# Six instead of three projection matmuls between a step's scores and its weighing

## The reference

```python
x = x + attn(layernorm(x), wq, wk, wv, wo)     # 32 heads of 64, 8 key/value heads, rotary, causal
x = x + xattn(layernorm(x), ctx_2048)          # both sides rounded to fp8 by blocks, then x @ ctx^T
x = x + moe(layernorm(x), Wg, W1, W3, W2, sw1, sw3, sw2)   # 8 experts, top 1, capacity 256, one shared
```

```python
xq, xk, xv = x @ wq, x @ wk, x @ wv            # then rotary on xq and xk
scores = einsum('bqhd,bkhd->bhqk', xq, xk) / 8, with a causal mask
out = einsum('bhqk,bkhd->bqhd', softmax(scores), xv) @ wo
```

## Time and profile before

| | |
|---|---|
| median of three runs | 1614.04 us (1612.98 to 1614.66) |
| the profiled execution | 1614.8 us, of which span 1613.0 us |
| mean granted TensorE clock | 0.956 of full speed (2.4 GHz) |
| TensorE matmul busy | 1467.1 us, 91% |
| VectorE / ScalarE / GpSimd busy | 1237.6 (77%) / 917.9 (57%) / 1058.6 us (66%) |
| attention, step 0 | from 51.73 us |
| steps 52 to 59 | 422.33 to 495.87 us |
| step 117 | from 912.21 us |

### The profile page before, as it was taken

One profiled execution on the slowest core, in us unless ns is written; L12 is line 12 of the kernel. 1 busy time (PEld: TensorE's weight loads), 2 busy tenths in 40 slices (PEclk: granted clock), 3 DMA queues, 4 the chain that ended last, 5 costly groups with the idle time before them and its releaser, 6 DMA issues.

```text
span 1613.0 us, 26858 instructions
## 1 busy us (share of the span) xinstructions
PE 1467.1 (91%) x8616; PEld 1290.2 (80%) x8616; DVE 1237.6 (77%) x2986; ACT 917.9 (57%) x2277; POOL 1058.6 (66%) x1040
## 2 busy tenths in 40 slices
PE   5899999999989999999999967728889898899997
PEld 4688888888878888888888856627778787899996
DVE  6787787788887787788787879858797964677785
ACT  2587777777667777777777655422121213566562
POOL 1798888888776888888888767626252522444545
PEclk9899999999999999999999988969989899899998
DMA  5322232222312222232322333031101003577767
GB/s 189 87 73 66 81 76 71 77 81 55 81 50 63 75 74 66 81 89 55 82 76 59 112 119 92 8 125 41 52 27 53 7 27 113 160 234 221 226 209 239
DMA packets 78796, 152.13 MB, mean 94 GB/s; under 512 B 15366, under 2 KB 15622, under 8 KB 78656
## 3 DMA queue, kind: packets, MB, share of 16 engines
q1 hardware_dynamic: 76096, 142.16, 30.3%
q0 software_dynamic: 2560, 8.25, 1.5%
HBM read 87.58 MB, written 16.78 MB: 65 GB/s over the span
## 4 chain that ended last, share of the span: by engine, by line
PE 74%; DVE 12%; issue 6%; POOL 4%; ACT 2%; DMA 1%; SPq 1%; DVEq 0%; POOLq 0%; ACTq 0%
PE bank L400 15%; PE bank L401 15%; PE bank L402 15%; PE bank L442 7%; PE bank L418 5%; PE bank L457 5%; PE bank L458 5%; PE bank L419 4%; PE bank L392 2%; DVE work L943 1%; POOL P L1390 1%; DVE work L1056 1%; DVE aam L1095 1%; PE bank L429 1%; DVE st L938 1%
## 5 line engine op out<-in xcount | busy, mean ns | idle before, releaser
L742 ACT ACTIVATE P<-P,mn 128x512 f32<-128x512 f32 (+3 forms) x512 | 284.5, 556 | 221.6 <-DVE mn L994 220.9
L1390 POOL TENSOR_TENSOR P<-P,ri 128x128 f32<-128x128 f32 (+3 forms) x512 | 353.9, 724 | 10.4 <-DVE ri L983 10.4
L994 DVE CUSTOM_DVE_ANT_0 P<-bank,mask 128x512 f32<-128x512 f32 (+3 forms) x512 | 235.6, 479 | 118.3 <-PE bank L419 117.9
L1035 DVE TENSOR_TENSOR PTl<-bank,PTh 128x512 fp32r<-128x512 f32 (+1 forms) x384 | 229.2, 598 | 37.0 <-ACT PTh L754 33.9
L442 PE MATMUL bank<-ident,P 128*128 128x128 f32 x1280 | 203.4, 274 | 7.2 <-POOL P L1390 7.2
L754 ACT ACTIVATE PTh<-bank 128x512 fp32r<-128x512 f32 (+1 forms) x384 | 197.6, 516 | 6.0 <-PE bank L442 2.9
L418 PE MATMUL bank<-KT,QT 128*128 128x256 f32 (+2 forms) x512 | 191.2, 373 | 7.4 <-DVE mn L994 7.3
L457 PE MATMUL bank<-PTh,VS 128*128 128x256 f32 (+2 forms) x512 | 164.5, 332 | 11.5 <-DVE PTl L1035 8.8
L400 PE MATMUL bank<-XT,Wh 128*128 128x512 f32 x384 | 165.4, 431 | 9.6 <-DVE qcs L1007 4.7
L419 PE MATMUL bank<-KT,QT 128*128 128x256 f32 (+2 forms) x512 | 167.3, 327 | 0.0
L1428 POOL TENSOR_TENSOR OTl<-Opair,OTh 128x512 fp32r<-128x512 f32 x64 | 83.5, 1305 | 120.8 <-ACT OTh L764 120.5
(11 more groups left out here) (190 smaller groups left out, 4214.5 us busy)
## 6 DMA issues: line engine op xcount, KB each, us to landing
RW<-in_wf SPq DMA_DIRECT2D x170, 256.0 KB, 3.2
QT<-qh SPq DMA_DIRECT2D x256, 64.0 KB, 2.0
QT<-ql SPq DMA_DIRECT2D x256, 64.0 KB, 2.0
Wraw<-in_wqkv SPq DMA_DIRECT2D x16, 768.0 KB, 4.8
Oraw<-in_wo SPq DMA_DIRECT2D x16, 512.0 KB, 3.4
KT<-KT SPq DMA_DIRECT2D x32, 256.0 KB, 2.9
work<-in_ctx SPq DMA_DIRECT2D x32, 256.0 KB, 2.7
krot<-kvs SPq DMA_DIRECT2D x64, 64.0 KB, 2.0
```

The lines of the kernel that those rows point to most:

```text
L742: e.activation(pq, pq, ACT.Exp, bias=mn[:, z, qb:qb + 1], scale=-1.0, accum_out=rs[:, z, qb:qb + 1]).then_inc(a_exp, 1)
L994: e.tensor_tensor_reduce(P[:, z, off[qb]:off[qb] + k], bank[n % 2][:, 0:k], mask[:, 512 - k:512], -0.125, BIG, ALU.add, ALU.min, mn[:, z, ...
L1035: e.tensor_tensor(pt_part(PTl, part), bank[2 + part][:, 0:128 * n].rearrange("p (m n) -> p m n", n=128), pt_part(PTh, part).bitcast(F32), ...
L1390: e.tensor_tensor(pq, pq, ri[:, z, qb:qb + 1].to_broadcast([128, n]), ALU.mult).then_inc(g_norm, 1)
```

## The change

Of the three projection chunks of a step, nine matmuls, the kernel before issues the first (three matmuls) between `scores(h, 2)` and `weigh(h - 3)`, and the other two (six matmuls) between `turn_p(h - 2, 2)` and `attn_out(h - 7)`. The changed kernel issues two chunks at the first place and one at the second. The order of the chunks among themselves, their waits, and the work of the other engines are as they were.

```diff
--- before.py
+++ after.py
@@ -636,7 +636,8 @@
                     scores(h, 3)
                     scores(h, 2)
                 if unit < NU:
-                    project(unit, 3 * k // 4, 3 * k % 4)
+                    for at in range(3 * k, 3 * k + 2):
+                        project(unit, at // 4, at % 4)
                 if 0 <= h - 3 < NH:
                     weigh(h - 3)
                 if h >= NH - 11:
@@ -656,8 +657,7 @@
                 if 0 <= h - 2 < NH:
                     turn_p(h - 2, 2)
                 if unit < NU:
-                    for at in range(3 * k + 1, 3 * k + 3):
-                        project(unit, at // 4, at % 4)
+                    project(unit, (3 * k + 2) // 4, (3 * k + 2) % 4)
                 if 0 <= h - 7 < NH:
                     attn_out(h - 7)
                 if h < -4:
```

## The result

| | before | changed |
|---|---|---|
| median | 1614.05 us (1612.98 to 1615.16, 6 runs) | 1621.01 us (1617.99 to 1623.38, 6 runs) |
| ratio, 95% interval | | 1.0043, 1.0031 to 1.0055 (+5.0 to +8.9 us) |
| the profiled execution | 1614.8 us, span 1613.0, clock 0.956 | 1623.38 us, span 1621.6, clock 0.951 |

The change makes the kernel 7.0 us slower.

What follows compares the result with a forecast made beforehand. TensorE, busy 91%, was taken as the bound, so a new order could only create or remove waits. The terms +0.6 - 1.2 + 2.6 + 0.1 + 0.7 = +2.8 us gave 1616.8 us; range 1611.0 to 1623.0.

Steps and rivals of the forecast that it cites:

- (a): Whole kernel: the forecast case, a small sum of terms of both signs, 1614 to 1620 us; chance 0.54.
- within 0.2%: Whole kernel: a change of at most 3.2 us, 1610.8 to 1617.3, hardly told from none; chance 0.51.
- (c): Steps with k = 1, 2, 3: `join` misses `attn_out`, 81 steps pay about 0.1 us, 1624.2 in all; chance 0.17.
- part 2: Every eighth step: `weigh` no longer waits for the X add, 12 x 0.10 = -1.2 us.
- part 1: `join` to `attn_out`: tightest margin falls from 0.94 to 0.25 us, 0.02 to 0.03 lost in 26 steps, +0.6 us.
- part 3: Steps 52 to 59: the later inner group delays VectorE's X add, for which `first_turn` waits; +2.6 us.
- rival (d): Steps 52 to 59: longer waits drop the clock to 1.2 GHz, about +5 us, 1621.8; chance 0.05.
- part 4: The start: 0.70 us won by matmuls ahead of a GpSimd wait, given back in steps 3 to 8; +0.1 us.
- part 5: The end, after step 119: the chain of waits follows the inner group, so 0.69 us is paid once; +0.7 us.
- Rival (b): Steps 52 to 59 and start: VectorE's slack swallows the lateness, the start keeps its gain; -2.6 us, 1611.4; chance 0.15.
- (e): Whole kernel: the order is hidden wherever it stands, TensorE being full; 1614.0 us; chance 0.09.

Runs made afterwards that it cites:

- experiment on both places: Against the kernel before: last three projection matmuls behind `attn_out` in steps 52-59 and every eighth quiet step, VectorE's add and normalising earlier in 52-59; 1607.47 us, ratio 0.9964.
- experiment on the waiting steps: Against the kernel before: six projection matmuls ahead only in steps whose `weigh` waits for the X add (and step 2); 1618.02 us, ratio 1.0033.

## Why the prediction was right, and where not

The sign was right, and 1621.0 lies inside the whole range (1611.0 to 1623.0). It lies 1.0 above what I gave to the forecast case (a), 1614 to 1620, and 4.2 above the 1616.8 that I named; "within 0.2%", to which I gave the best chance (0.51), did not come. That the range held owes something to luck: its upper end was drawn for (c) and for a clock at half speed, and what filled it was a spacing and a late copy that stood in no term, beside a small fall of the clock. The terms, each from the profiles:

| term | predicted | measured |
|---|---|---|
| part 2, waits of `weigh` | -1.2 | -1.2 |
| part 1, what the new order costs in quiet steps | +0.6 | +2.8 |
| part 3, steps 52 to 59 (step 56 from least to least) | +2.6 | +2.2 |
| rival (d), the clock | in no sum | 1.4 to 1.6 in two of three profiles, about +1.0 |
| part 4, step 2 and steps 3 to 8 | +0.1 | +0.16 |
| the copy of the keys | in no sum | about +1.1 at step 0 (the copy itself +1.3 to +1.8) |
| part 5, the end | +0.7 | +0.5, not told from nothing |
| sum | +2.8 | about +6.6 |

Measured as a whole: +7.0 and +6.8 us. The four experiments that change one stage each sum to 2.4 + 1.8 + 2.9 - 0.1 = +7.0, of which 0.5 is the return to the old order at step 51. Each of the four is uncertain by some 1.5 us, so that they meet the whole this closely is in part luck.

**Part 1 failed in its size and in its reason.** The margins came out as worked out (0.25 predicted, 0.24 measured for k = 2), `attn_out` lost nothing by them, and rival (c) did not occur. I charged the 26 steps with the tightest margin 0.02 to 0.03 us each and put the rest at nothing. Steps with k = 0, whose margin is 0.82, take 7.74 instead of 7.70, those with k = 1 7.17 instead of 7.11 to 7.14, and the others 7.14 and 7.12 instead of 7.11: the quiet stages take +0.76 and +0.92 us (+1.6 together on average over three profiles), and with the 1.2 that part 2 gives back that is +2.8. What pays most of it is TensorE's spacing: in three kinds of step `attn_out`'s matmuls stand 0.233 us apart and not 0.228 to 0.229, which is 0.024 us a step or 1.8 us in all. The rest is spread over the step's other matmuls, most of it over the four of `scores` 3 and 2 (0.01 to 0.015 us a step where k = 0, 1 or 2). The spacing of `attn_out` does not follow VectorE's weight splits: in the step with k = 0 VectorE splits weights in every second unit only, and the spacing is the same in both. In the kind with the tightest margin (k = 2) it is the narrow one. Six or nine matmuls between the transposes and `attn_out` go with the narrow spacing throughout. Three go with the wide one in three kinds of step, but not for k = 2, and with both in the experiment on both places. So TensorE's sequence has a part in it and can't be the whole cause; the mechanism stays open. My condition for being wrong, "if quiet steps without a wait take another time than 7.1 us", was met by a few hundredths, and a few hundredths in 98 steps came to 2.8 us where I had 0.6.

The Trainium skill, "TensorE: Matmul & The Clock Gate", section "Back-to-back issue gap", gives between matmuls of 512 columns about 216 ns for one alone and about 131 ns in a stream, and no number by place. No such pair in these rows is under 0.22 us, and the 0.005 us between one place in the order and another is what counted here.

**Part 2 was right**: 7.14 us for step 18, no late matmul in `weigh`. The experiment on the waiting steps adds what the prediction left out: the gain holds only while the next step has the new order too.

**Part 3 was right by step**, 52 to 55 and 57 to 59 within 0.07 us. Step 56 costs +0.67 for +0.69 where its split is equally long, and +0.28 from least to least, since in two of the three profiles with the new order the split no longer ran beside a GpSimd instruction. I had not looked at that. The waits of `first_turn` sum to 10.9 us in the changed kernel (11.8 predicted) and to 11.9 where the split was long. The longest was to be in step 56; in the changed kernel it is the one of step 54 (1.65), and step 56 has 1.05:

```profile
PE bank L392 <- DVE X L1044: 10.9, 8, 1.6
```

That VectorE's chain sets these steps, which the +0.45 rested on, is shown by its reversal: moving the add forward in that chain gained 6 us.

**Rival (d)**, given 0.05, occurred in small, in two of three profiles: half the speed for 3.4 us, 1.4 to 1.6 us lost and not 5.

**Part 4 was right in both halves** (-0.67 for -0.70, +0.83 for +0.8) and incomplete. I followed TensorE, GpSimd and VectorE, and no DMA. The copy of the keys is late in all three profiles with the new order up to step 8 and in none of the eleven others, with a packet of instructions among its own packets each time; in the others that packet comes from 37.8 us on, behind the copy. The rest of the attention says the same: of the 64 KB copies of keys (krot) and queries (QT from qh) before 900 us, 3148 had no packet of instructions (8 KB or more) in their time, and all but one of them took 1.89 to 2.06 us; 1018 had one, and took up to 3.97, with medians of 2.3 and 2.4. So a packet among its own is what makes such a copy late. What moves the packet is open, since the one step that I blamed did not do it.

**Rival (b)** (VectorE's slack swallows the delay) and **(e)** (hidden everywhere) are out: the waits grew.

## What to carry to other kernels

When the engine that is full has its work reordered, price each place by what the *other* engine on the loop does: moving TensorE's matmuls alone won 1.6 us at best here and cost up to 89, and moving VectorE's X add and normalising with them won 5.6 us. Where a stage repeats a hundred times, compare whole steps of the same kind across margins, not only the margins: 0.03 us a step is 3 us. A reorder in some steps only can be paid again where the old order comes back (0.47 us here behind each waiting step, nothing behind step 59), so try it as a block. An instruction that is longer in one profile than in another is not chance until one has looked at what the other engines do beside it.

## What the runs showed of the hardware

- Matmuls of the same shape on a full TensorE at clock 1.00 do not all have one spacing: in `attn_out` it is 0.225 to 0.236 us by their place, and the mean of the six mostly repeats within 0.001 us from step to step (0.228 to 0.229 in the order before, 0.233 in three of four kinds of step in the changed one). What sets it is open.
- Instructions are fetched by the same DMA engines as data, 0.02 MB a packet; with one among its packets the first unit's 64 KB copy of keys took 3.24, 3.25 and 3.76 us instead of 1.97, and of 3148 like copies without one a single one took more than 2.06 (2.25). The Trainium skill, "Runtime: NRT & Kernel Launch", section "Instruction fetch mechanics", has blocks of 16 KiB, which agrees, and calls their cost mostly hidden, which these copies do not bear out.
- The granted clock fell from 2.4 to 1.2 GHz for 3.4 us, behind waits of 1.38 and 0.80 us in one profile and 1.38 and 0.64 in another, and not behind waits of 1.38 and 2.09 us in a third, nor behind others of up to 1.65 in the same two.
- VectorE's weight split (two inputs, neither in a bank) is held up by GpSimd's two-input instructions on krot and kt: started beside one, it ended 0.55 us behind that one's end in 165 of 172 cases, and took up to 1.78 us instead of 0.68. On the critical chain, as in step 56, that moves the whole kernel by as much.
